# Skipping clamped rows in the indirect gathers of a recommender kernel

## The reference

```python
emb = emb_tables[jnp.arange(26)[:, None], x_cat]         # 26 tables of 12500 rows of 64 floats; 2048 samples
feats = jnp.concatenate([transpose(emb), dense_embed[:, None, :]], axis=1)
gram = jnp.einsum('bid,bjd->bij', feats, feats)
concat = jnp.concatenate([gram[:, _IU, _JU], dense_out], axis=1)
out = (jax.nn.relu(concat @ Wt1 + bt1) @ Wt2 + bt2)[:, 0]
```

## Time and profile before

| what | value |
|---|---|
| median of 3 runs | 541.75 us (541.12 to 544.3) |
| span of the profiled execution | 540.9 us |
| POOL busy / PE / ACT / DVE | 393.8 / 291.1 / 246.8 / 190.2 us |
| gathers on POOL | 416, mean 944 ns |
| granted TensorE clock, mean | 0.719 of full speed |

### The profile page before, as it was taken

One profiled execution on the slowest core, in us unless ns is written; L12 is line 12 of the kernel. 1 busy time (PEld: TensorE's weight loads), 2 busy tenths in 40 slices (PEclk: granted clock), 3 DMA queues, 4 the chain that ended last, 5 costly groups with the idle time before them and its releaser, 6 DMA issues.

```text
span 540.9 us, 6578 instructions
## 1 busy us (share of the span) xinstructions
PE 291.1 (54%) x1932; PEld 234.6 (43%) x1932; DVE 190.2 (35%) x672; ACT 246.8 (46%) x816; POOL 393.8 (73%) x425
## 2 busy tenths in 40 slices
PE   0027465382744638466382644727275372786785
PEld 0017354271533517255271533616154261574564
DVE  3016043160613416053160612516043160612553
ACT  0127255271734527265281733637255281733653
POOL 6777777777777777777777777777777777777750
PEclk9997758576585856667567685767758586588888
DMA  6333332333333333333333333333332333332110
GB/s 186 27 26 30 25 27 26 27 26 26 26 27 26 27 26 27 25 26 26 26 27 26 27 27 25 27 26 27 26 26 26 27 26 26 26 26 26 29 23 1
DMA packets 14345, 16.07 MB, mean 30 GB/s; under 512 B 7169, under 2 KB 7425, under 8 KB 14209
## 3 DMA queue, kind: packets, MB, share of 16 engines
q0 software_dynamic: 13312, 13.66, 31.2%
q1 hardware_dynamic: 578, 2.19, 1.1%
q10 hardware_dynamic: 448, 0.14, 0.1%
HBM read 15.95 MB, written 0.01 MB: 29 GB/s over the span
## 4 chain that ended last, share of the span: by engine, by line
POOL 70%; issue 26%; PE 1%; ACT 1%; DMA 1%; POOLq 1%; DVE 0%
POOL gathered L191 70%; PE ps_mlp L432 1%; ACT gram L129 1%; DMA gathered<-in_table,tile_idx 1%; DMA raw_idx<-in_x_cat 0%; POOLq L185 0%; PE ps_gram L414 0%; POOLq L40 0%; POOLq L189 0%; PE ps_mlp L425 0%; PE ps_mlp L440 0%; DVE feats L154 0%; DVE top L336 0%; ACT scores L249 0%; PE ps_trans L383 0%
## 5 line engine op out<-in xcount | busy, mean ns | idle before, releaser
L191 POOL DMA_INDIRECT gathered<-in_table,tile_idx x416 | 392.7, 944 | 128.6 <-issue 126.5
L383 PE MATMUL ps_trans<-ident,gathered 128*128 128x128 f32 x208 | 50.1, 370 | 189.9 <-DMA gathered<-in_table,tile_idx 189.0
L129 ACT COPY gram<-ps_gram 32x56 f32<-32x56 f32 x512 | 131.1, 256 | 41.9 <-PE ps_gram L414 35.2
L129 DVE COPY gram<-ps_gram 32x56 f32<-32x56 f32 x512 | 130.1, 254 | 54.4 <-PE ps_gram L414 46.6
L414 PE MATMUL ps_gram<-feats 64*128 64x128 f32 x1024 | 112.8, 395 | 38.1 <-ACT feats L139 18.2
L414 PEld LDWEIGHTS ps_gram<-feats 64*128 64x128 f32 x1024 | 102.4, 295 | 49.2 <-DVE gram L129 25.5
L139 DVE COPY feats<-ps_trans 64x256 f32<-64x256 f32 (+1 forms) x120 | 45.3, 378 | 218.4 <-PE ps_trans L383 217.2
L383 PEld LDWEIGHTS ps_trans<-ident,gathered 128*128 128x128 f32 x208 | 30.5, 180 | 205.8 <-issue 148.3
L219 ACT CAST tile_idx<-row_idx 128x8 uint32 (+3 forms) x61 | 12.0, 196 | 203.3 <-PE ps_trans L383 202.7
L432 PE MATMUL ps_mlp<-gram,wt1p_sb 128*128 128x128 f32 x448 | 69.6, 317 | 18.1 <-ACT gram L129 14.9
L432 PEld LDWEIGHTS ps_mlp<-gram,wt1p_sb 128*128 128x128 f32 x448 | 63.4, 225 | 24.1 <-DVE gram L129 21.5
(11 more groups left out here) (26 smaller groups left out, 56.6 us busy)
## 6 DMA issues: line engine op xcount, KB each, us to landing
gathered<-in_table,tile_idx POOLq DMA_INDIRECT x416, 3.3
price_bc<-in_price SPq DMA_DIRECT2D x1, 1024.0 KB, 5.7
wt1p_sb<-in_wt_pairs SPq DMA_DIRECT2D x1, 896.0 KB, 8.3
raw_idx<-in_x_cat SPq DMA_DIRECT2D x1, 195.0 KB, 3.2
w_sb<-in_w ACTq DMA_DIRECT2D x2, 32.0 KB, 5.4
wt1d_sb<-in_wt_dense ACTq DMA_DIRECT2D x1, 64.0 KB, 8.2
consts_sb<-in_consts ACTq DMA_DIRECT2D x1, 4.5 KB, 2.0
raw_idx<-in_x_cat SPq DMA_DIRECT2D x1, 13.0 KB, 1.8
```

What stands on the lines that cost most here:

```text
L129: last = copy(gram_to[QUAD * c:QUAD * (c + 1), :, RG * r:RG * (r + 1), :, s], gram_from[r % 2][QUAD * s:QUAD * (s + 1), :, :, s, 0:SLABS, c])
L191: pool.indirect_dma_start(out=gathered[:, f * D:(f + 1) * D], out_offset=None, in_=rows, in_offset=bass.IndirectOffsetOnAxis(ap=tile_idx[: ...
L383: last = nc.tensor.transpose(ps_trans[c % 2][:, k * P:(k + 1) * P], gathered[:, f * D:(f + 2) * D], ident[:, :])
```

## The change

Each tile gets a gather buffer of its own in `gathered` (16 times 26 fields). A new tensor `last_rows` holds the last row of each table in every partition; SP loads it from the tables. SP then copies it into the buffers of tiles 1 to 15, one buffer after the other, each waiting for the one before (`filled`); the last tile's buffer has its fields in another order and takes four smaller copies. DVE adds 1048576 to the row number of every clamped id of tiles 1 to 15 (`beyond`, `row_at`), and every gather gets a bound, `TABLE_END` = 324999: an index above it is skipped, and what stands in the buffer stays. Tile 0 has no prefilled buffer and its row numbers stay as they are. The row numbers are integers in one tensor `row_idx` from which the gathers read directly, so the copies into `tile_idx` on ACT and their signal go. Before each tile after the first, POOL waits for the buffer's fill, and before each chunk for the landing of that chunk of the tile before. The loops on all engines are written out.

```diff
+            last = table[:, LAST_ROW, :].rearrange("(o f) d -> o f d", o=1).to_broadcast([P, FIELDS, D])
+            sp.dma_start(last_rows[:, :].rearrange("p (f d) -> p f d", d=D), last).then_inc(last_loaded, 16)
             sp.dma_start(price_bc[:, :], price.rearrange("(o b) -> o b", o=1).to_broadcast([P, BATCH])).then_inc(price_loaded, 16)
             sp.dma_start(wt1p_sb[:, :], wt1_pairs).then_inc(pairs_loaded, 16)
+
+            sp.wait_ge(last_loaded, 16)
+            for t in range(1, TILES - 1):
+                sp.dma_start(gathered[:, t * ROW:(t + 1) * ROW], last_rows[:, :]).then_inc(filled, 16)
+                sp.wait_ge(filled, 16 * t)
...
-            with pool.Fori(0, TILES) as t:
+            for t in range(TILES):
+                if t == 0:
+                    pool.wait_ge(rows_made, 1)
+                else:
+                    pool.wait_ge(rows_made, 3)
+                    pool.wait_ge(filled, 16 * t if t < TILES - 1 else 16 * (t - 1 + TAIL_FILLS))
                 for c, (f0, f1) in enumerate(CHUNKS):
-
-                    pool.wait_ge(tile_idx_set[c], t + 1)
-                    pool.nop(nofuse=True)
+                    if t > 0:
+
+                        pool.wait_ge(chunk_gathered[c], 16 * (f1 - f0) * t)
                     for f in range(f0, f1):
-                        pool.indirect_dma_start(out=gathered[:, f * D:(f + 1) * D], out_offset=None, in_=rows,
-                                                in_offset=bass.IndirectOffsetOnAxis(ap=tile_idx[:, f:f + 1], axis=0))\
+                        at = t * FIELDS + f
+                        pool.indirect_dma_start(out=gathered[:, at * D:(at + 1) * D], out_offset=None, in_=rows,
+                                                in_offset=bass.IndirectOffsetOnAxis(ap=row_idx[:, at:at + 1], axis=0),
+                                                bounds_check=TABLE_END, oob_is_err=False)\
                             .then_inc(chunk_gathered[c], 16)
...
-                if next_indices:
-                    nc.scalar.copy(tile_idx[:, f0:f1], row_idx[:, bass.ds((t + 1) * FIELDS + f0, f1 - f0)])\
-                        .then_inc(tile_idx_set[c], 1)
...
+            step(nc.vector.tensor_scalar(beyond[:, a:e], clamped[:, a:e], float(LAST_ROW), float(OUTSIDE),
+                                         ALU.is_ge, ALU.mult))
+            step(nc.vector.tensor_tensor(row_at[:, a:e], clamped[:, a:e], beyond[:, a:e], ALU.add))
```

More of the change, by code:

```diff
@@ L28 @@
 NPAIR = SLOTS * (SLOTS - 1) // 2
+ROW = FIELDS * D
+LAST_ROW = VOCAB - 1
+TABLE_END = FIELDS * VOCAB - 1
+OUTSIDE = 1 << 20
+TAIL_FILLS = 2 * UNITS
 WP, BP, B1, B2, BT1, WT2, BT2 = 0, 1, 2, 3, 4, 6, 8
@@ L56, in rec_kernel @@
         clamped = sb("clamped", [P, TILES * FIELDS])
-        row_idx = sb("row_idx", [P, (TILES + 1) * FIELDS])
-        tile_idx = sb("tile_idx", [P, FIELDS], u32)
-        gathered = sb("gathered", [P, FIELDS * D])
+        beyond = sb("beyond", [P, TILES * FIELDS])
+        row_at = sb("row_at", [P, TILES * FIELDS])
+        row_idx = sb("row_idx", [P, TILES * FIELDS], u32)
+        last_rows = sb("last_rows", [P, ROW])
+        gathered = sb("gathered", [P, TILES * ROW])
         feats = sb("feats", [P, HALF, PAD])
@@ L90, in rec_kernel @@
         rows_made = sem("rows_made")
+        last_loaded = sem("last_loaded")
+        filled = sem("filled")
         small_loaded = sem("small_loaded")
@@ L162, in _ @@
             sp.dma_start(raw_idx[:, FIELDS:], x_cat[:, FIELDS:]).then_inc(idx_loaded, 16)
+            last = table[:, LAST_ROW, :].rearrange("(o f) d -> o f d", o=1).to_broadcast([P, FIELDS, D])
+            sp.dma_start(last_rows[:, :].rearrange("p (f d) -> p f d", d=D), last).then_inc(last_loaded, 16)
             sp.dma_start(price_bc[:, :], price.rearrange("(o b) -> o b", o=1).to_broadcast([P, BATCH])).then_inc(price_loaded, 16)
             sp.dma_start(wt1p_sb[:, :], wt1_pairs).then_inc(pairs_loaded, 16)
+            sp.wait_ge(last_loaded, 16)
+            for t in range(1, TILES - 1):
+                sp.dma_start(gathered[:, t * ROW:(t + 1) * ROW], last_rows[:, :]).then_inc(filled, 16)
+                sp.wait_ge(filled, 16 * t)
+            for q in range(2):
+                part = slice(HALF * q, HALF * (q + 1))
+                of_half = last_rows[part, :].rearrange("p (f q d) -> p f q d", q=2, d=D)[:, :, q, :]
+                for u in range(UNITS):
+                    at = (TILES - 1) * ROW + u * (ROW // UNITS)
+                    sp.dma_start(gathered[part, at:at + ROW // UNITS].rearrange("p (f d) -> p f d", d=D), of_half)\
+                        .then_inc(filled, 16)
             sp.wait_ge(score_stored, TILES + 1)
@@ L209, in dense_features, with odd_fields @@
             def dense_features(dst, part, first, n, t):
-                return nc.scalar.activation(dst, price_bc[part, bass.ds(t * P + first, n)], ACT.Identity,
+                return nc.scalar.activation(dst, price_bc[part, t * P + first:t * P + first + n], ACT.Identity,
                                             bias=const(BP, part), scale=const(WP, part))
-            def odd_fields(c, t, next_indices=True, evacuate=evacuate_chunk):
-                f0, f1 = CHUNKS[c]
+            def odd_fields(c, t, evacuate=evacuate_chunk):
                 act.wait_ge(chunk_transposed[c], t + 1)
-                if next_indices:
-                    nc.scalar.copy(tile_idx[:, f0:f1], row_idx[:, bass.ds((t + 1) * FIELDS + f0, f1 - f0)])\
-                        .then_inc(tile_idx_set[c], 1)
                 evacuate(nc.scalar.copy, c, 1).then_inc(trans_evac_act, 1)
@@ L248, in store_scores @@
                 act.wait_ge(score_summed, t + 1)
-                nc.scalar.activation(scores[:, bass.ds(t * P, P)], ps_score, ACT.Identity,
+                nc.scalar.activation(scores[:, t * P:(t + 1) * P], ps_score, ACT.Identity,
                                      bias=const(BT2, slice(0, 1))).then_inc(score_stored, 1)
@@ L267, in _ @@
             tile(0, first=True)
-            with act.Fori(1, TILES - 2) as t:
+            for t in range(1, TILES - 2):
                 tile(t)
@@ L273, in _ @@
             dense_parts(t)
[L274 removed]
+            odd_fields(1, t, evacuate_unit_chunk)
             hidden_relu(t)
@@ L306, in _ @@
             dve.wait_ge(base_made, 3)
[L307 to L309 removed]
+            nc.vector.tensor_tensor(row_idx[:, 0:FIELDS], clamped[:, 0:FIELDS], field_base[:, :], ALU.add)\
+                .then_inc(rows_made, 1)
             dve.wait_ge(idx_loaded, 16)
             clamp(FIELDS, TILES * FIELDS)
[L312 removed]
+            a, b, e = FIELDS, (TILES - 1) * FIELDS, TILES * FIELDS
+            step(nc.vector.tensor_scalar(beyond[:, a:e], clamped[:, a:e], float(LAST_ROW), float(OUTSIDE),
+                                         ALU.is_ge, ALU.mult))
+            step(nc.vector.tensor_tensor(row_at[:, a:e], clamped[:, a:e], beyond[:, a:e], ALU.add))
             nc.vector.tensor_tensor(row_idx[:, a:b].rearrange("p (t f) -> p t f", f=FIELDS),
[L314 removed]
+                                    row_at[:, a:b].rearrange("p (t f) -> p t f", f=FIELDS),
                                     field_base[:, :].rearrange("p (o f) -> p o f", o=1)
                                     .to_broadcast([P, TILES - 2, FIELDS]), ALU.add).then_inc(rows_made, 1)
[L317 removed]
+            nc.vector.tensor_tensor(row_idx[:, b:e], row_at[:, b:e], last_base[:, :], ALU.add)\
                 .then_inc(rows_made, 1)
[L319 removed]
             nc.vector.memset(feats[:, :, :], 0.0).then_inc(feats_zeroed, 1)
@@ L347, in _ @@
             even_fields(0, 0)
-            with dve.Fori(0, TILES - 2) as t:
+            for t in range(TILES - 2):
                 tile(t)
@@ L368, in keep_warm @@
             def keep_warm(t, place, bank):
-                if isinstance(t, int) and t in WARM and place > 0:
+                if t in WARM and place > 0:
                     for _ in range(WARM[t][place - 1]):
@@ L383, in transpose_chunk @@
                     last = nc.tensor.transpose(ps_trans[c % 2][:, k * P:(k + 1) * P],
-                                               gathered[:, f * D:(f + 2) * D], ident[:, :])
+                                               gathered[:, t * ROW + f * D:t * ROW + (f + 2) * D], ident[:, :])
                 last.then_inc(chunk_transposed[c], 1)
@@ L396, in gram_rounds @@
             def gram_rounds(t, rounds, chunks):
-                if chunks == NC and isinstance(t, int):
+                if chunks == NC and t in WARM:
                     pe.wait_ge(trans_evac_dve, NC * t + NC + 1)
@@ L458, in _ @@
             tile(0, first=True)
-            with pe.Fori(1, TILES - 2) as t:
+            for t in range(1, TILES - 2):
                 tile(t)
```

6 lines of the change are left out of this document (2 added, 4 removed).

## The result

The changed kernel takes 563.6 us (median; 562.51 to 564.28) against 542.16 us for the kernel before it (541.12 to 544.3, four runs, three of which are those of the table ahead): a ratio of 1.0387, 95% interval 1.0367 to 1.0406. It is slower, and the forecast of 396 us was wrong in sign.

What follows compares the result with a forecast made beforehand. POOL's gathers were taken as the bound. First gather at 4.3 us, 26 x 1.248 for tile 0, 15 x 22.7 for the other tiles, 17.5 behind them and 0.85 around gave 396 us; range 335 to 580 us.

Steps and rivals of the forecast that it cites:

- What bounds the kernel: POOL's gather stream: 416 gathers, one every 1.248 us, 519.1 us of the 540.9 us span; PE, DVE and ACT follow.
- The term that decides: A bounded gather on POOL: 0.84 of its 0.944 us taken as row cost, so skipping changes the time by -145.6 us.
- x: Share of a row's cost in a POOL gather that skipping saves; taken as 0.6, the change being -242.6 us times it.
- The rival "slower": In all 416 POOL gathers, a per-row bound test adds 0.089 us each, 37 us, giving 579 us; chance 0.26.
- The first rival: A gather's time on POOL does not depend on skipped rows: no gain, 541.75 us within 1 us; chance 0.19.
- The terms near nothing: ACT copies, DVE operations, last_rows load, fills, landing waits and register setting: each taken as 0 us.
- The floor: Compute of a tile on PE, ACT and DVE, below POOL's beat: some 19.5 us a tile if nothing waits for gathers.

## Why the prediction was wrong

*What bounds the kernel* was right: POOL's beat, and 416 times any change in it. 416 x 53 ns = 22.0 us against 21.4 us between the medians.

*The term that decides* failed, in the step that took 0.10 us as the fixed part of a gather from the smallest POOL instructions. A memset of one column is no gather: by the line through the runs with fewer rows the fixed part is 0.83 us, and 128 rows hold 0.12 us, not 0.84. Even had each skipped row given back its whole 0.92 ns, 330 x 112 of them would have been worth 34 us and not 242.6. The second error lay in x: I took 0.6 of a row's cost as saved, and measured 0, since gathers with no row to fetch take the same 997 ns. And the bound itself, which the sum had at nothing, costs 53 ns a gather; that is the whole of the slowdown. No row of the trace before could have settled the fixed part: its 416 gathers are within a few ns of each other, but all have 128 rows. For want of such a row I gave a comparison with instructions of another kind more weight than it could bear.

*The Trainium skill's rule* ("DMA: Bandwidth & Descriptors", "Anatomy of one DMA"), that descriptor generation is small and variable and many can be emitted before the cost shows, stands up: 0.92 ns a row beside 0.83 us. I had it in hand and gave it the smaller chance. The Trainium skill's figure ("GPSIMD Engine Reference", section 3.1) of about 12 cycles an element for a data-dependent branch isn't seen: the bound costs 53 ns over 128 rows, 0.4 ns each even if all of it is laid on the rows.

*The rival "slower"* had the right place, inside all 416 gathers, tile 0 as long as the rest, and the right sign; its price of 89 ns was 53, and most of it is paid once a gather, not for each row. The result lies inside the range of 335 to 580 us only because this rival's price set the upper end. The first rival named a part of the cause in passing, that skipped rows are still worked off in some form (4 bytes each on the queue).

*The terms near nothing* were right together (ratio 1.0009 without the bound), with sizes off: `last_rows` landed in 6.6 us, not 10.5; a fill in 3.9 us, not 8; PE's first transposes start at 18.75 us, 2 us later and not 4 to 5; the register's 29 ns stay under the gather ahead, and the gap is 0.30 us as forecast. The bytes of queue 0 (4.33 MB, forecast 4.2) were right and beside the point; their share of the queues' time fell further, to 5.1% where the first rival had some 9. I had called the part behind the last gather fixed at 17.5 us; it lost 2.0 in this trace, 1.6 of them by a clock that the next run of the kernel need not get. PE's wait for gathers was to shrink to 50 us and grew to 215.5.

*The floor* of 19.5 us a tile was never reached and stays untested.

## What to carry to other kernels

Where an engine that makes transfers is the bound, ask for the price of one instruction and of one row apart, by asking for fewer rows, before saving rows: here it is 0.83 us and 0.9 ns, so by these figures only fewer gathers would help (no run tried that). Skipped rows unburden the DMA queue (5.1% of its time for 31.2%), which I would expect to pay where landings are waited for; here it was their issue. A fixed part is not to be read off an instruction of another kind, nor off instructions that all have the same number of rows: it takes a run in which that number changes.

## What the runs showed that was not expected

On the slow chips the order of kernels turned. The written-out kernel without the bound took 1.1398 times the kernel before (one execution of it even 1381.64 us), while the looped kernel with the bound took 0.9956 of it; on the other chips the ratios are 1.0009 and 1.0398. POOL's gathers were no longer than elsewhere at the median (947 and 1000 ns), though in the written-out kernel without the bound 167 of them took over 1.05 us. POOL's beat was not the bound there: in the looped kernel POOL waited 176.4 us for ACT's copies of row numbers, and in the written-out one it was done at 561 us. It was PE, ACT and DVE that stood still there, for up to 77, 54 and 87 us at a time, and PE's matmuls came singly, as in this timeline of PE in the written-out kernel without the bound:

```profile
130.97 0.37 PE L408 MATMUL ps_trans<-ident,gathered 128*128 128x128 f32 x1 [1.24 <-issue]
133.78 0.37 PE L408 MATMUL ps_trans<-ident,gathered 128*128 128x128 f32 x1 [2.43 <-issue]
136.56 0.37 PE L408 MATMUL ps_trans<-ident,gathered 128*128 128x128 f32 x1 [2.42 <-issue]
138.67 0.37 PE L408 MATMUL ps_trans<-ident,gathered 128*128 128x128 f32 x1 [1.73 <-issue]
```

Four transposes that stand together elsewhere are 2.1 to 2.8 us apart, and the trace shows nothing that they wait for. Why, and why the kernel with written-out code, fills and wide buffers suffers more there, stays open; no run told these apart.
